# Four small register loads in place of two large ones on TensorE: attention and a routed feed-forward, one core

## The reference, cut to what matters

```python
x = L0_attn_input_data                                   # (2, 2048, 128)
xn = _layernorm(x, axis=-1)
scores = jnp.einsum('bsd,de,bte->bst', xn, qk, xn) / SCALE    # causal mask, softmax -> attn
attention = jnp.einsum('bst,btd,de->bse', attn, xn, ov)
eid = jnp.argmax(xn @ centroids.T, axis=-1)              # the expert of each token
h = jax.nn.relu(xln @ w1[e] + b1[e])                     # xln: xn normalised again, by the expert's gain and bias
ffn = onehot[:, e:e + 1] * (h @ w2[e] + b2[e])           # summed over the 8 experts
x = x + attention + (xn + alpha * ffn)
```

## Time and profile before

| | us |
|---|---|
| median of 3 runs | 224.81 |
| lowest and highest | 223.13, 225.4 |
| span of the profiled execution | 223.1 |

### The profile page before, as it was taken

How to read it: one execution, slowest core, us unless ns; L and a number is a source line. 1 busy time by engine, 2 the same in 40 slices (tenths; PEclk the granted TensorE clock), 3 DMA queues, 4 the chain that set the end, 5 groups by cost and what they waited for, 6 DMA issues and landing times.

```text
span 223.1 us, 6878 instructions
## 1 busy us (share of the span) xinstructions
PE 206.3 (92%) x2428; PEld 159.9 (72%) x2428; DVE 175.5 (79%) x448; ACT 155.2 (70%) x346; POOL 154.3 (69%) x230
## 2 busy tenths in 40 slices
PE   7699776999979999999999999799999999999993
PEld 5544323768856875777766889799999996787773
DVE  6588999899899999999999875556448575535995
ACT  2639989784578899777748755646665658868781
POOL 6173759994259999989999338998999899960000
PEclk9859999999999999999999999999999999999999
DMA  6992003397001111111111696536683111116964
GB/s 167 314 289 64 6 0 94 116 355 232 5 12 39 36 39 39 44 43 40 36 40 36 128 198 160 125 92 141 131 150 92 50 40 37 38 35 172 256 193 141
DMA packets 37601, 23.55 MB, mean 106 GB/s; under 512 B 12472, under 2 KB 34144, under 8 KB 37568
## 3 DMA queue, kind: packets, MB, share of 16 engines
q1 hardware_dynamic: 34960, 18.28, 32.3%
q0 software_dynamic: 2272, 4.69, 6.3%
q10 hardware_dynamic: 336, 0.14, 0.3%
HBM read 11.17 MB, written 9.38 MB: 92 GB/s over the span
## 4 chain that ended last, share of the span: by engine, by line
PE 77%; DVE 11%; ACT 4%; issue 4%; DMA 2%; SPq 1%; DVEq 0%; ACTq 0%
PE psum L1343 6%; PE psum L1300 6%; PE psum L1301 6%; PE psum L1302 6%; PE psum L1351 6%; PE psum L1344 6%; PE psum L1277 5%; PE psum L1460 4%; PE psum L1461 4%; PE psum L1462 4%; PE psum L1434 4%; PE psum L1436 4%; PE psum L1435 4%; PE psum L1260 3%; PE psum L1334 2%
## 5 line engine op out<-in xcount | busy, mean ns | idle before, releaser
L910 DVE TENSOR_TENSOR p_lo<-p_sb,p_hi 128x512 f16<-128x512 f32 (+1 forms) x68 | 42.0, 638 | 12.2 <-ACT p_sb L1050 12.0
L1044 ACT ACTIVATE p_hi<-psum 128x512 f16<-128x512 f32 (+1 forms) x68 | 37.1, 547 | 19.4 <-PE psum L1351 14.2
L1050 ACT ACTIVATE p_sb<-psum 128x512 f32<-128x512 f32 (+1 forms) x80 | 42.5, 539 | 6.8 <-PE psum L1334 6.7
L693 POOL DMA_INDIRECT sorted_y<-xn x39 | 38.1, 977 | 11.6 <-ACT xn L1174 5.5
L1018 DVE SCALAR_TENSOR_TENSOR h_lo<-psum,h_hi 128x512 f16<-128x512 f32 x39 | 26.8, 690 | 21.5 <-ACT h_hi L1166 18.7
L671 POOL MEMSET v_full<- 1x600 f32 x71 | 41.7, 588 | 0.0
L684 POOL DMA_INDIRECT sorted_x<-xr,pos x32 | 33.5, 1047 | 11.9 <-issue 11.4
L1166 ACT ACTIVATE h_hi<-psum 128x512 f16<-128x512 f32 x39 | 23.3, 597 | 21.0 <-PE psum L1436 19.2
L1343 PE MATMUL psum<-v_hi,p_hi 128*128 128x129 f16 x236 | 32.7, 220 | 1.2 <-DVE x_sb L927 1.2
L896 DVE TENSOR_REDUCE row_max<-psum 128x1 f32<-128x512 f32 x48 | 32.3, 682 | 1.6 <-PE psum L1277 1.1
L1344 PE MATMUL psum<-v_lo,p_hi 128*128 128x128 f16 x236 | 32.6, 219 | 0.0
(11 more groups left out here) (189 smaller groups left out, 528.4 us busy)
## 6 DMA issues: line engine op xcount, KB each, us to landing
w_raw<-in_L_ffn_w SPq DMA_DIRECT2D x16, 256.0 KB, 4.2
sorted_x<-zero SPq DMA_DIRECT2D x3, 780.0 KB, 6.4
xn<-sorted_x SPq DMA_DIRECT2D x8, 260.0 KB, 3.9
x_sb<-in_L_attn_input_data SPq DMA_DIRECT2D x8, 256.0 KB, 5.6
xn<-sorted_y SPq DMA_DIRECT2D x8, 256.0 KB, 4.9
out<-x_sb SPq DMA_DIRECT2D x6, 256.0 KB, 3.3
sorted_y<-xn POOLq DMA_INDIRECT x39
sorted_x<-xr,pos POOLq DMA_INDIRECT x32
```

The lines of the kernel that those rows point to most:

```text
L693: pool.indirect_dma_start(out=sorted_y[:, :], out_offset=bass.IndirectOffsetOnAxis(ap=tokens, axis=0), in_=xs[:, t % SLOTS, 0:P], in_offse ...
L910: v.tensor_tensor(p_lo[:, u, off:GW], p_sb[:, u, off:GW], p_hi[:, u, off:GW], ALU.subtract).then_inc(s_plo, 1)
L1044: a.activation(p_hi[:, u, off:GW], bank[SCORE[n % R]][:, off:GW], ACT.Exp, scale=SCALE).then_inc(s_exph, 1)
L1050: a.activation(p_sb[:, u, off:GW], bank[SCORE[n % R]][:, off:GW], ACT.Exp, scale=SCALE).then_inc(s_exp, 1)
```

## The change

The 39 numbers are loaded in four lots, at four entries of the table: REG.0 where REG was (in front of M.1.2.2.1), REG.1 behind P.33, REG.2 behind PB.34, REG.3 behind P.36. The bounds are 0, 9, 19, 29 and 39, so the lots have 9, 10, 10 and 10 numbers. Each waits for s_tile_e, as REG did. `hidden` loads nothing any more.

```diff
-X.35 PB.31 PB.32 REG M.1.2.2.1 P.33 M.1.2.1.0 SH.1.1 P.34 X.36 PB.33 P.35 PB.34 X.37 M.1.2.0.2 M.1.2.1.2 PB.35 P.36
+X.35 PB.31 PB.32 REG.0 M.1.2.2.1 P.33 REG.1 M.1.2.1.0 SH.1.1 P.34 X.36 PB.33 P.35 PB.34 REG.2 X.37 M.1.2.0.2 M.1.2.1.2 PB.35 P.36 REG.3
...
-    FIRST_EXPERTS, LOAD_REST = 20, 12
+    LOTS = 4
...
                 if kind == "REG":
                     pe.wait_ge(s_tile_e, 1)
-                    load_experts(0, FIRST_EXPERTS)
+                    first, end = job[1] * NS // LOTS, (job[1] + 1) * NS // LOTS
+                    load_experts(first, end - first)
...
                 m.then_inc(s_z, 1)
-                if k == LOAD_REST:
-                    load_experts(FIRST_EXPERTS, NS - FIRST_EXPERTS)
```

## The result

The changed kernel takes 227.79 us in the median of 4 runs (226.99 to 229.72), the kernel before 224.70 us on the same chip. The ratio is 1.0159, 95% interval 1.011 to 1.0208: slower by 3 to 3.5 us. A second measurement, later, gave 1.0156 (1.0111 to 1.020). The prediction was 223.5 us, within 1% of before, with a range up to 225.1 and a chance of 0.05 for slower. It was wrong in sign and in size.

The account below looks back on a forecast made before the run. PE was taken to bound the kernel, busy 206.3 of 223.1 us, with holes at both register loads. Feed-forward -1.31 us plus attention 0.0 gave -1.3, from the median 224.81 to 223.5 us, range 221.7 to 225.1.

Parts of the forecast that it names:

- the cost of one lot: Attention loads: a lot of 10 registers takes 0.78 us, in proportion to the first load's 1.555 us for 20.
- sign of a wrong unit: Profile after: a load row lasting over 1 us would show the 78 ns a register to be wrong.
- rival on the slow side: Attention loads: time does not depend on count; 1.555 to 1.874 us a lot gives 225.9 to 227.2 us; chance 0.07.
- The second load leaves the feed-forward: Feed-forward: PE's 1.31 us hole behind the second load goes, and nothing else makes PE wait there: -1.31 us.
- a rest that others used: Feed-forward hole: ACT, x2T transfers or POOL's stores bring the 1.31 us back later; time stays 224.8 us; chance 0.1.
- The sequencer's rule: Attention: a load stops PE's sequencer, not its queue; the sequencer cannot pass a semaphore an earlier product still waits for.
- The stage comes out even: Attention: 0.47 us lost at the first load becomes about 0.40 at the third lot; net -0.06 to +0.05 us.
- The hole of 0.4 us that I saw ahead of X.37: Attention, third lot: its load behind PB.34 waits for DVE and ends at 104.85 us, leaving PE a 0.4 us hole.
- The sum, -1.3 us: Whole kernel: -1.31 us in the feed-forward plus 0.0 in the attention, from a median of 224.81 to 223.5 us.
- its dearest case: Attention: every lot takes 1.874 us whatever its count, net +2.4 us, 227.2 us.
- A large fixed part: Attention: a lot has a fixed part or feed-forward register cost; kernel gains 1.05 us, 223.8 us; chance 0.18.
- all lots are hidden: Attention: XL.34 comes earlier or lots take under 0.4 us, saving 0.47 us too: -1.78, 223.0 us; chance 0.08.

Follow-up runs that it names:

- slots of their own: Changed kernel, same counts (9, 10, 10, 10), VectorE writing the lots to start at entries 0, 12, 24 and 36: 222.01 us, ratio 0.9931 to the kernel before.
- cut at multiples of four: Changed kernel with its four lots cut at entries 8, 20 and 28, not 9, 19 and 29: 221.93 us, ratio 0.9944 to the kernel before.
- GpSimd's pair early: Changed kernel with lots from entries 0, 8, 16, 24, 32, eight entries each, and GpSimd's last three pauses left out: 222.76 us, ratio 0.9954 to before.
- five lots: Changed kernel with lots of 8 entries from 0, 8, 16, 24, 32, the last at an added place in the attention: 223.11 us, ratio 0.9958 to before.

## Why the prediction was wrong

The step that failed is **the cost of one lot**: "In proportion it is 1.555 x 10/20 = 0.78 at the first load's rate", and the bound above it, "no dearer than the dearest whole load, 1.874". The lots of ten took 2.44 to 2.65 us. A load's price is not a rate times a count: by the table it is 0.24 to 0.33 us for each fetch, and where the run starts decides whether a fetch brings four entries or one. Both loads of before start at multiples of four, so no row of that trace could show the dear case; the bound assumed that a part costs no more than the whole. The prediction's own sign of a wrong unit, a load row over 1 us, showed in all four rows. Two smaller terms stood at nothing in the sum: the fall of TensorE's clock behind a long hole, and the p_lo that GpSimd's pair holds, 1.43 and 0.78 us in the two profiles of the changed kernel.

Two rows did hint at it. Nineteen registers took longer than twenty, which I noted and put down to the DMA share; it is 4 + 3 single fetches against 5. And the Trainium skill (Runtime: NRT & Kernel Launch, section Instruction fetch mechanics) gives some 200 ns a register, which I set aside because 20 registers had taken 1.555 us. That figure is for loads from HBM. The runs, whose table lies in SBUF, come near it where a load starts off a multiple of four, at 241 to 265 ns an entry; at multiples of four 8 entries take 0.59 us, 74 ns each. By its rule a lot of ten would have been 2.0 us, an estimate that lies above the 1.27 us from which my rival on the slow side decides.

Point by point:
- *The second load leaves the feed-forward, -1.31 us, and nothing else is due there.* Right: 65.85 to 64.50 us, PE busy for all of it. The hole was the load and not a rest that others used.
- *The sequencer's rule.* Right. With lots near the assumed price (slots of their own) the second, third and fourth lot start 1.26, 3.95 and 5.50 us after the first; I had 0.91, 3.97 and about 5.3. The product behind the second lot starts 0.17 us after its load's end after the change as well (102.02 to 102.19).
- *The stage comes out even.* Nearly right had the lots been so cheap: cut at multiples of four or in slots, with loads of 0.6 to 1.3 us, it costs 0.3 to 0.4 us more; with 0.6 us (and GpSimd's pair early) it saves 0.35. The hole of 0.4 us that I saw ahead of X.37 did not come there (0.10 us or less behind the third lot). Holes came behind the second lot (0.23 and 0.68 us) and the fourth (0.55 and 0.14), where I had none.
- *The sum, -1.3 us.* It is about what the change brings with its cuts at multiples of four or in slots: 0.9931 to 0.9944, that is 1.25 to 1.5 us. Their stretches give 1.0 (1.35 less 0.3 or 0.4), so the closeness is in part luck.
- *The rival on the slow side* had the right sign, and its threshold of 1.27 us a lot was passed by far. Its mechanism, a price independent of the count, was wrong (0.59 us for 8, 0.98 for 12), and its dearest case, +2.4 us, was still too cheap for the 3 to 3.5 measured.
- *The other rivals.* A large fixed part is out: 8 entries take 0.59 us and 12 take 0.86. That all lots are hidden did not need lots under 0.4 us, as I had it: five lots of 0.6 to 0.8 us leave 0.10 us or less behind each.
- *The profiled execution.* I set the span of 223.1 us to the run of 223.13. In all later runs the time lies 1.7 to 1.8 us above the span of its own profile (228.47 and 226.7 after), so that execution was one of nearly 225 us. As the forecast was given from the median, this moved nothing.

## What to carry to other kernels

Before a table of numbers is read into registers in pieces, put the pieces' first entries at multiples of 16 bytes (cut there, or pad the table) and make their counts multiples of four: here entries 9 to 18 cost 2.65 us in one profile and 2.48 in another, 8 to 19 cost 0.98. A price per unit from two rows holds for the shapes of those two rows; before cutting a transfer, ask what else the cut changes (its start, its remainder), and take no whole for the upper bound of its parts. A load that TensorE's sequencer has to wait for hides if it is shorter than the queue of products ahead of it. Here that queue was 0.6 to 1.0 us long at the second and the fourth place and in the feed-forward, and 1.3 at the first. So small pieces at several places lose less than large ones: 0.10 us or less behind each of five, 0.46 and 1.05 behind two. (The medians of those two kernels do not tell them apart.)

## What the runs showed of the hardware

- TensorE's granted clock falls to 0.50 (1.2 GHz) at some holes in these stages: at 2.16, 2.37 and 4.44 us, not at 2.02, 1.60, 1.56 or 1.40 us in these profiles. No run varied the length of a hole alone, so no threshold is shown. The products that followed ran at half speed for 3.2 us (after the 2.16 us hole) and 5.0 us (after 4.44 us). Just ahead of the fall, in the changed kernel, 0.81 us of products still ran at 1.00; in the hole of 4.44 us it came 1.7 us before the next product. Far ahead of the loads, between 8 and 17 us, the clock is at 0.50 for a while in nine of the thirteen profiles, before included, and in four, the changed kernel's two among them, not at all. The latest first loads, at 99.1 to 100.1 us, are all in profiles of the nine; that is one reason why the stage starts at different times.
- VectorE's p_lo (f32 less f16 to f16) and GpSimd's subtraction of two 512-column tiles do not run side by side: p_lo lasts 1.4 to 3.7 us in place of 0.69 and ends 0.55 us after GpSimd's second product in the profiles. A row_max of 0.69 us at 121.24 in the kernel before ran beside the pair at its usual length; it reads PSUM, p_lo reads two tiles of SBUF. The Trainium skill (SBUF — State Buffer, section SBUF: two separate sides) has a rule for this: a VectorE operation with two SBUF inputs and a GpSimd operation that reads SBUF take turns on one pair of ports, and whichever starts first keeps it for its whole instruction while the other stands still. The traces agree in that p_lo is held until the pair is done; that the first to start wins they do not show in the five lots, where the held p_lo's row begins 0.9 us before GpSimd's first product. What it costs PE depends on where it falls: 0, 0.8 or 1.3 to 1.4 us. Part of the changed kernel's loss in its first profile (1.43 us) is this; whether the stage's delay brought it about stays open, since a profile of the kernel before has it too.
